# A two-layer top-2 mixture-of-experts kernel: the GpSimd queue sends a step's results back before it fetches rows four steps on, and a scratch area for running sums moves

## The reference

```
x = x + 0.5 * ffn(layernorm(x))
x = x + attention(layernorm(x))      # 16 heads, no softmax: (q k^T) v, with rotary q and k
x = x + 0.5 * ffn(layernorm(x))      # the same weights again

ffn:  logits = x @ router                       # 8 experts
      top 2 experts per token, weights w = softmax of the two logits
      gate, up = split(x @ gate_up[e] + bias)   # 256 -> 512, even and odd columns
      act = (clip(up) + 1) * gate * sigmoid(1.702 * gate)
      out = sum over the two experts of w * (act @ down[e] + bias)
```

## Time and profile before

| | us |
|---|---|
| median of 3 runs | 738.54 (736.97 to 738.88) |
| the profiled execution | 740.95 |
| its span | 739.1 |
| PE busy in the span | 609.8 |
| POOL busy in the span | 411.9 |
| expert steps of layer 0, first to last POOL transfer | 96.3 to 300.4 |
| expert steps of layer 1, first to last POOL transfer | 500.0 to 701.9 |

### The profile page before, as it was taken

The page is one execution under the profiler, slowest core; times in us unless marked ns, Lnnn a source line. Parts: engine busy times, 40 slices in busy tenths (PEclk is TensorE's granted clock), DMA queues, the critical chain, the costliest instruction groups (busy, mean ns, idle before and its releaser), DMA issues.

```text
span 739.1 us, 13830 instructions
## 1 busy us (share of the span) xinstructions
PE 609.8 (83%) x3900; PEld 538.8 (73%) x3901; DVE 455.2 (62%) x1130; ACT 360.4 (49%) x800; POOL 411.9 (56%) x444
## 2 busy tenths in 40 slices
PE   3782489999999999788997799459999999999700
PEld 3781378888888888767776799448888888888600
DVE  4557946555555555388885588684555555555356
ACT  4884424545455554378875244233454555554300
POOL 2445555777777774369996100007577777776400
PEclk9999999999999999999999899659999999999955
DMA  9675032322333331434431442113222333222189
GB/s 324 226 212 168 1 117 77 92 98 92 98 98 98 99 92 52 142 117 140 158 101 58 142 158 100 57 1 91 77 92 94 98 99 98 93 95 78 50 313 369
DMA packets 52018, 88.01 MB, mean 119 GB/s; under 512 B 15634, under 2 KB 31425, under 8 KB 51468
## 3 DMA queue, kind: packets, MB, share of 16 engines
q1 hardware_dynamic: 21334, 43.69, 17.9%
q0 software_dynamic: 13664, 35.42, 15.3%
q10 hardware_dynamic: 16982, 8.43, 3.9%
HBM read 53.96 MB, written 35.39 MB: 121 GB/s over the span
## 4 chain that ended last, share of the span: by engine, by line
PE 62%; DVE 12%; DMA 9%; POOL 7%; ACT 5%; issue 4%; SPq 1%; ACTq 0%; DVEq 0%; POOLq 0%
PE ps L820 15%; PE ps L822 15%; PE ps L821 15%; PE ps L811 10%; DMA work<-y_dram 4%; PE ps L815 3%; POOL aT_lo L523 2%; PE ps L838 2%; DMA xn_dram<-work 2%; DVE xs L1349 1%; DVE work L1263 1%; POOL xn_lo L517 1%; ACT work L566 1%; POOL work L513 1%; POOL work L514 1%
## 5 line engine op out<-in xcount | busy, mean ns | idle before, releaser
L484 POOL DMA_INDIRECT y_dram<-work,sidx x142 | 143.1, 1008 | 73.5 <-issue 42.2
L476 POOL DMA_INDIRECT work<-xn_dram,gidx x142 | 145.9, 1028 | 46.6 <-issue 42.5
L811 PE MATMUL ps<-cst,work 128*128 128x128 f32 x824 | 133.4, 288 | 26.9 <-ACT work L566 21.5
L811 PEld LDWEIGHTS ps<-cst,work 128*128 128x128 f32 x824 | 104.7, 150 | 40.4 <-issue 14.0
L820 PE MATMUL ps<-up_hi,xT_hi 128*128 x284 | 118.1, 416 | 1.0 <-DVE xT_lo L1293 1.0
L822 PE MATMUL ps<-up_hi,xT_lo 128*128 x284 | 112.1, 395 | 0.0
L821 PE MATMUL ps<-up_lo,xT_hi 128*128 x284 | 111.9, 394 | 0.0
L670 ACT ACTIVATE work<-ps 128x256 f32<-128x256 f32 x142 | 54.7, 385 | 108.0 <-PE ps L822 108.0
L1308 DVE TENSOR_SCALAR work<-ps 128x256 f32<-128x256 f32 x142 | 59.8, 421 | 65.6 <-ACT work L670 65.0
L679 ACT ACTIVATE work<-ps,slot_gate 128x256 f32<-128x256 f32 x142 | 59.8, 472 | 81.2 <-PE ps L822 81.2
L1290 DVE SCALAR_TENSOR_TENSOR slot_gate<-work,sign,second 128x1 f32<-128x1 f32 x142 | 25.5, 219 | 101.5 <-ACT xT_hi L656 101.5
(11 more groups left out here) (157 smaller groups left out, 1406.1 us busy)
## 6 DMA issues: line engine op xcount, KB each, us to landing
work<-y_dram SPq DMA_DIRECT2D x32, 512.0 KB, 5.0
xs<-L_attn_x SPq DMA_DIRECT2D x4, 1024.0 KB, 10.0
work<-L_ffn_gate_up_proj SPq DMA_DIRECT2D x8, 512.0 KB
q_dram<-work ACTq DMA_DIRECT2D x16, 256.0 KB, 2.7
work<-q_dram SPq DMA_DIRECT2D x16, 256.0 KB, 2.7
out<-xs SPq DMA_DIRECT2D x16, 256.0 KB, 5.9
xn_dram<-work SPq DMA_DIRECT2D x16, 255.0 KB, 3.7
xn_dram<-work ACTq DMA_DIRECT2D x16, 255.0 KB, 2.2
```

The costliest lines, as they stand in the source:

```text
L476: pool.indirect_dma_start(xg[:, k, u, 1:H + 1], None, xn_dram[n], bass.IndirectOffsetOnAxis(ap=gidx[:, 2 * s + u:2 * s + u + 1], axis=0)). ...
L484: pool.indirect_dma_start(y_dram[n], bass.IndirectOffsetOnAxis(ap=sidx[:, 2 * s + u:2 * s + u + 1], axis=0), ysb[:, k, u, :], None, bounds ...
L811: ins = nc.tensor.transpose(ps[:, bank, k:k + P], src[:, u, c * P:(c + 1) * P], ident)
```

## The change

Two edits. In POOL's loop over the steps, the scatter of s-2 now stands ahead of the gather of s+4, together with its wait for `y_sb`. The first four gathers and the last two scatters stay where they are. And `running` starts at word 1024 of `work` instead of word 6208. No wait, no instruction and no transfer is added or taken away.

```diff
-        running = area(6208, 2, PAD + NT, E, dt=BF16)
+        running = area(1024, 2, PAD + NT, E, dt=BF16)
...
                 for s in range(RING):
                     gather(s)
                 for s in range(NP):
+                    if s >= 2:
+                        scatter(s - 2)
                     if s + RING < NP:
                         pool.wait_ge(l.x_lo, s + 1)
                         gather(s + RING)
-                    if s >= 2:
-                        scatter(s - 2)
                 for s in range(NP - 2, NP):
                     scatter(s)
```

## The result

| | before | after |
|---|---|---|
| median of 20 runs each, us | 738.92 (735.58 to 742.01) | 741.03 (739.02 to 743.54) |
| ratio | | 1.0025, 95% interval 1.0014 to 1.0037 |
| span of the profiled execution, us | 739.1 | 739.4 |

The change makes the kernel slower by a quarter of a per cent, some 1.9 us. That is inside the 0.3% that I had called "no difference", and inside the range, but with twenty runs on each side it is a real difference and the forecast of exactly 0 us was not right. The two single spans differ by 0.3 us only; single executions of one kernel spread over more than that (735.58 to 742.01 before), so the spans don't show where the 1.9 us are. The timelines show where PE loses time.

What follows compares the result with a forecast made beforehand. The prediction took PE to bound the kernel, with POOL just keeping pace. Its terms summed to 740.95 + 0 + 0 + 0 = 740.95 us for the profiled execution, so a median of 738.6 us, range 736.0 to 741.2.

Steps and rivals of the forecast that it cites:

- no difference: Whole kernel: a difference of 0.3%, 2.2 us, is about what can be told from none; chance 0.84.
- What bounds the kernel: Expert stages: PE sets the 5.32 us step, and POOL keeps pace with almost nothing to spare.
- The alternation stays, no scatter moves: POOL's queue from the first scatter on: same alternation of two scatters and two gathers, scatters unmoved, 0 us.
- The gathers become one step later, 4.45 us remain: Gathers in POOL's queue: 4.45 us from the second gather's start to PE's use, landing 2.9 us; taken 0 us.
- a ceiling of 1.25 us for a late landing: Gathers: the ramp's longest landing, 5.7 us, less the 4.45 us lead, would cost 1.25 us once in a layer.
- one lost landing in each layer: Late-gather case: one lost landing in each layer gives 741.1 us, so the range was taken to 741.2.
- the slack: Gathers: lead of 4.45 us less the landing, 1.55 us in the median and 0.35 in the worst case seen.
- A delay of one landing is absorbed and not passed on.: Round of gather, PE and scatter over three steps: allows 4.80 us a step at a 2.9 us landing.
- The end of the gathers: End of a layer: scatter of step 29 starts 0.3 us late, step 30's and later ones stay; 0 us.
- The running sums: Eight DVE instructions at another word offset, 2.28 us a layer: 0 us taken, bounds -0.8 to +1.4 us.
- Gathers come too late: Rival at PE's transposes: landings over 4.45 us make PE wait; 743.6 us, or 764 if all are 5.7; chance 0.08.
- The two pages: Gathers: one page's fit gives 2.3 us landing, slack 2.15; the other delays transfers during DVE operations; both add 0.

Runs made afterwards that it cites:

- run 10: Changed kernel with POOL's old order (gather, then scatter) from step 20 on; ratio 0.9998 to the kernel before at 738.54 us.
- run 9: Changed kernel with `running` back at word 6208, so POOL's new order alone; ratio 1.0028 to the kernel before at 738.54 us.
- run 2: Kernel before with only `running` moved to word 1024, POOL's old order kept; ratio 1.0001 to the kernel before at 822.19 us.
- run 3: Same kernel as run 10, old order from step 20 on; ratio 1.0042 to the kernel before at 822.19 us.
- run 5: Kernel before, old order, with five memsets on POOL ahead of step 12's gather; ratio 1.0036 to the kernel before at 833.47 us.
- run 11: Same kernel as run 5, old order with five memsets on POOL; ratio 0.9995 to the kernel before at 836.49 us.
- split order: Changed kernel with each in-loop scatter split: first tile, then both gathers, then second tile; run 4 ratio 0.9976, run 8 ratio 1.0090.
- run 8: Changed kernel with the scatter's two tiles split around the gathers; ratio 1.0090 to the kernel before at 833.47 us.
- run 4: Same kernel as run 8, scatter split around the gathers; ratio 0.9976 to the kernel before at 822.19 us.
- run 1: Same kernel as run 9, POOL's new order alone; ratio 1.0009 to the kernel before at 822.19 us.
- run 6: Changed kernel with five memsets on POOL at step 12's place in the loop; ratio 1.0052 to the kernel before at 833.47 us.
- run 12: Same kernel as run 6, changed kernel with five memsets on POOL; ratio 1.0030 to the kernel before at 836.49 us.
- run 7: Same kernel as run 9, POOL's new order alone; ratio 1.0088 to the kernel before at 833.47 us.

## Why the prediction was right, and which term was not

- **What bounds the kernel.** PE, with POOL just as full: right. PE is full in every stretch in which the gathers come in time, before, after and in run 10.
- **The alternation stays, no scatter moves.** Right to the tenth up to the 113th transfer: idle time of 8.20 us against 8.2 forecast, then the same rhythm.
- **The gathers become one step later, 4.45 us remain.** Right as a number: with the second gather of step 6 at 124.96 and PE's transposes 0.38 us later than before, the lead is again 4.45. But the step then said "Taken: 0 us", against a ceiling of 1.25 us for a late landing, and this is the term that was mis-sized. It measured 0.96 us in layer 0 and 1.06 us in layer 1. That the total still fell inside the range is in part luck: the range's upper end came from one lost landing in each layer, and what happened was another thing, of like size. I had weighed the slack against landings alone, one at a time, from 1.55 us in the median to 0.35 in the worst case. The landings of 3.6 to 3.9 us, which I took for rare worst cases, are the rule in a layer's last steps, so the slack there was some 0.7 us and not 1.55. And I had taken POOL's rhythm as fixed. The slack has to pay for everything that can make POOL late, and since POOL is full, for the sum of it: of the 1.4 us that POOL lost at once it had won back only 0.1 when the gathers ended. The gap of 1.4 us did not exist in the trace of before; together with the landings of 3.8 to 4.1 us at the end of the layer, much like those of before, it went over the slack.
- **"A delay of one landing is absorbed and not passed on."** Right for a single late landing, and the wrong question: a gap in POOL's own queue shifts all later gathers.
- **The end of the gathers.** Forecast 0.3 us late for S29, with S30 on time. Beyond the 0.38 us that stood at S0, S29 is 1.6 us late (276.50 against 274.51), S30 0.7 (280.87 against 279.82), and S31 to S35 are 1.0 late, which is what PE lost (the last one 300.71 against 299.37).
- **The running sums.** 0 us, right in the profile: 0.17, 0.23, 1.59 and 0.29 us again.
- **The rivals.** "Gathers come too late" was the right mechanism, with its place and its sign in the profile. Its point of decision, a landing of 4.45 us, was never reached: the longest landing of these gathers was about 4.1. The lateness came from before the start of the gather.
- **The two pages.** The Trainium skill (DMA: Bandwidth & Descriptors, anatomy of one SWDGE transfer) gives a landing of 2.3 us for this size, an estimate from its fit. The traces of before and after have 2.7 to 4.1 in one queue and one size once the scatters run, all above the fit, and a slack worked out from it would have been larger still and the forecast more sure of itself. By the Trainium skill (SBUF — State Buffer, the box on the trap that VectorE blocks a DMA) a gap would last as long as a DVE operation; DVE's operations around the gap last up to 0.7 us, the gap 1.4 to 1.55. So the rows don't bear it out as the cause.

**What stays open.** What the gap at the 114th transfer is. It stands at the same transfer of both layers, 1.42 and 1.55 us over the usual 0.30 in the changed kernel and 1.43 and 1.55 in run 9. In both, this transfer is the second tile of a scatter. Where it is a gather, the gap was 0 and 0.17 us in the kernel before and 0 in run 10. In runs 2, 3, 5 and 11 the 114th transfer, a gather, had 0.17 to 0.26 us too, and the five memsets with their waits ahead of it in runs 5 and 11 didn't move that. In the split order it is also a gather, with 0.26 and 0.36 us in run 8, and in run 4 with none in layer 0 and 0.77 in layer 1; so a larger gap doesn't need a scatter everywhere. In runs 1, 6 and 12 it is a scatter and there was no gap, in run 7 one of 1.18 us in layer 1 only, where another transfer, the 121st, had 0.97 too; POOL has real waits in every second step there, so something that POOL owes may be paid in them, but that is a guess. No transfer of the instruction queues lies between 220 and 284 us in the changed kernel's trace, so a late load of code is not seen. Nor was it tried whether the gap alone, with the old lead, would be free where steps take 5.32 us; the old order's slack of 6.9 us says so, and that is argued, not shown.

## What to carry to other kernels

When two engines are full at once, the lead of one over the other is the only thing that keeps a hiccup of the first from the second, and a reorder that costs no instruction can still spend that lead. Add up all that may make the feeding queue late, gaps in its own issue too, and not only the longest transfer, and compare the sum with the lead that is left. Where nobody awaits the write-backs soon, fetches ahead of them keep that lead for nothing; here it was 5.32 us.

## What the runs showed of the hardware that was not expected

- A gap of 1.4 to 1.55 us in GpSimd's queue at one fixed transfer of a layer, the 114th. In the four traces with 5.32 us steps it stands only where that transfer is a scatter, and is at most 0.17 us where it is a gather; run 4 had 0.77 us at a gather.
- The same indirect gather of 128 rows of 1 KB lands mostly 2.7 to 2.9 us after its start in the middle of a layer (4.1 at most) and 3.5 to 3.9 us after it in a layer's last steps, in the kernel before and in run 10 alike.
- GpSimd's four transfers take 5.32 us a step in every arrangement in which it is full: of the two kinds, a first transfer after a change takes 1.10 us in one phase against the engines and 0.99 in another, and another transfer of the step takes the difference. After a gap of 1.4 us it kept this rhythm and won back only 0.1 us. Right after a wait for ACT in run 12 the same four transfers took 5.20 us (302.38 to 307.58), so full doesn't quite mean at its fastest.
- The same program took 738 us in some groups of runs and 822 to 836 in others, with hold-ups of ACT of mostly 1.7 to 4.7 us each, for much of which the traces give no releaser. It doesn't go with the chip number of the record: number 10 had both.
